# Products of every tile pair taken one pair later, with seven products for pair 0 as well, in an adaptive FFN kernel on one core

## The reference, cut to what matters

```python
# x: (32, 64, 1024) = 2048 tokens; W: (1024, 1024); A, B: 8 experts of rank 16; U, V: (1024, 256); S: (256,)
logits = x @ Wr.T + 5.0 * one_hot(ids)                     # 8 experts
gates  = softmax of the two largest logits, put at their places
h      = einsum('btd,erd->bter', x, A)
cond   = x @ W.T + 2.0 * einsum('bter,bte,eor->bto', h, gates, B)
out    = x + cond @ (U * S @ V.T).T
```

## Time and profile before

| | us |
|---|---|
| median of 3 executions | 155.24 (155.18 to 155.56) |
| the profiled execution, its own time | 154.92 |
| its span, first to last instruction | 153.1 |
| TensorE busy in the span | 148.8 (97%) |
| VectorE, GpSimd, ScalarE busy | 102.5, 67.2, 62.9 |

### The profile page before, as it was taken

How to read it: one execution, slowest core, us unless ns; L and a number is a source line. 1 busy time by engine, 2 the same in 40 slices (tenths; PEclk the granted TensorE clock), 3 DMA queues, 4 the chain that set the end, 5 groups by cost and what they waited for, 6 DMA issues and landing times.

```text
span 153.1 us, 2896 instructions
## 1 busy us (share of the span) xinstructions
PE 148.8 (97%) x1059; PEld 140.4 (92%) x1059; DVE 102.5 (67%) x291; ACT 62.9 (41%) x139; POOL 67.2 (44%) x53
## 2 busy tenths in 40 slices
PE   7999999999999999999999999999999999999991
PEld 5899999999998899899989998999899999989880
DVE  0787896945739997864884488267917782786551
ACT  4758783658626612812360335124511631230100
POOL 2000326015296650099129904970695089309000
PEclk9999999999999999999999999999999999999999
DMA  5999999996240059826198639765810680061084
GB/s 169 379 407 404 399 409 412 409 404 249 81 122 19 0 168 348 250 100 234 48 330 256 195 137 293 235 161 217 284 51 0 274 274 4 4 274 66 25 314 143
DMA packets 10669, 32.72 MB, mean 214 GB/s; under 512 B 1440, under 2 KB 1952, under 8 KB 10528
## 3 DMA queue, kind: packets, MB, share of 16 engines
q1 hardware_dynamic: 10368, 31.96, 58.1%
q10 hardware_dynamic: 288, 0.59, 1.0%
HBM read 24.16 MB, written 8.39 MB: 213 GB/s over the span
## 4 chain that ended last, share of the span: by engine, by line
PE 97%; DVE 0%; issue 0%; POOL 0%; DVEq 0%; POOLq 0%
PE fin L325 13%; PE fin L326 13%; PE fin L327 13%; PE pj L326 10%; PE pj L325 10%; PE pj L327 10%; PE zt L326 6%; PE zt L325 6%; PE zt L327 6%; PE fin L502 2%; PE gt L413 1%; PE zt L396 1%; PE fin L342 1%; PE gt L326 1%; PE gt L327 1%; PE gt L325 1%
## 5 line engine op out<-in xcount | busy, mean ns | idle before, releaser
L285 POOL TENSOR_TENSOR xT_lo<-xt_raw,xT_hi 128x1024 fp32r<-128x1024 f32 x16 | 38.2, 2407 | 67.3 <-DVE gh L762 32.9
L325 PE MATMUL pj<-proj_hi,xT_hi 128*128 128x264 f32 x128 | 36.4, 284 | 0.0
L326 PE MATMUL pj<-proj_lo,xT_hi 128*128 128x264 f32 x128 | 36.3, 284 | 0.0
L327 PE MATMUL pj<-proj_hi,xT_lo 128*128 128x264 f32 x128 | 36.2, 283 | 0.0
L325 PE MATMUL fin<-v_hi,w_hi 128*128 128x256 f32 (+1 forms) x84 | 26.4, 314 | 0.0
L326 PE MATMUL fin<-v_lo,w_hi 128*128 128x256 f32 (+1 forms) x84 | 26.3, 314 | 0.0
L327 PE MATMUL fin<-v_hi,w_lo 128*128 128x256 f32 (+1 forms) x84 | 26.3, 313 | 0.0
L300 POOL TENSOR_TENSOR x_all<-x_all,vw_raw 128x512 f32<-128x512 f32 x18 | 23.0, 1312 | 6.6 <-DVE vw_raw L810 6.6
L326 PEld LDWEIGHTS pj<-proj_lo,xT_hi 128*128 128x128 f32 x128 | 24.1, 188 | 0.2
L325 PEld LDWEIGHTS pj<-proj_hi,xT_hi 128*128 128x128 f32 x128 | 24.1, 188 | 0.2
L327 PEld LDWEIGHTS pj<-proj_hi,xT_lo 128*128 128x128 f32 x128 | 24.0, 188 | 0.0
(11 more groups left out here) (93 smaller groups left out, 288.0 us busy)
## 6 DMA issues: line engine op xcount, KB each, us to landing
xt_raw<-in_xt SPq DMA_DIRECT2D x16, 512.0 KB, 4.4
x_all<-in_x SPq DMA_DIRECT2D x16, 512.0 KB, 4.5
out<-x_all SPq DMA_DIRECT2D x13, 512.0 KB, 3.6
vw_raw<-in_VW SPq DMA_DIRECT2D x6, 384.0 KB, 7.0
w_raw<-in_W SPq DMA_DIRECT2D x8, 256.0 KB, 6.0
out<-x_all SPq DMA_DIRECT2D x5, 256.0 KB, 2.0
w_raw<-in_U SPq DMA_DIRECT2D x1, 1024.0 KB, 7.2
aw_raw<-in_AW SPq DMA_DIRECT2D x1, 544.0 KB, 7.2
```

Of the source, the lines that this page charges most:

```text
L285: nc.gpsimd.tensor_sub(xT_lo[:, t % XTR, :, :], xt_raw[:, t % XTR, :, :], xT_hi[:, t % XTR, :, :].bitcast(F32)).then_inc(xt_lo, 1)
L325: nc.tensor.matmul(dst, l_hi, r_hi, start=first, stop=False, skip_group_check=shared)
L326: nc.tensor.matmul(dst, l_hi, r_lo, start=False, stop=False, skip_group_check=shared)
L327: return nc.tensor.matmul(dst, l_lo, r_hi, start=False, stop=last, skip_group_check=shared)
```

## The change

All products move one pair later. While pair p runs, TensorE now issues `first_part(p-2)` between the two projections and `second_part(p-2)` after the second, then `half_t(p)` and `transpose_gh(p)`; `mix(p)` stands inside `project(2p+2)`, after five of its eight steps. Pair 0 has seven products like the others, so its `sums` and its differences of U S are needed too. At the end `first_part(6)`, `mix(7)` and `second_part(6)` follow the last `transpose_gh`, with `mix(7)` behind p1 and p6. The other engines' lists follow, and in the head the splits of x, B and U S stand at other places.

```diff
         LAST = TILES - 1
         PAIRS = TILES // 2
-        FAST = PAIRS - 2
-        HEAD_PRODS = 2 * HALF
+        LAG = 4
...
-                    if t == 2 and k == MH:
-                        mix(0)
+                    if t >= 2 and t % 2 == 0 and k == MH:
+                        mix(t // 2 - 1)
...
             for p in range(1, PAIRS):
                 project(2 * p)
-                if p >= 3:
+                if p >= 2:
+                    first_part(p - 2)
+                project(2 * p + 1)
+                if p >= 2:
                     second_part(p - 2)
-                project(2 * p + 1)
-                if p == 1:
...
-                    expand(0, bank_a, 0, 0, BANK)
-                    expand(0, bank_b, 0, BANK, D)
-                    pe.wait_ge(zb_lo, 1)
-                    expand(0, bank_c, MC, 0, BANK)
-                    expand(0, bank_d, MC, BANK, D)
-                else:
-                    first_part(p - 1)
-                transpose_gh(p)
                 zt_free(p)
                 half_t(p)
-                mix(p)
+                transpose_gh(p)
 
             p = PAIRS - 2
             q = (PAIRS - 1) % 2
+            p1(p)
+            p6(p)
+            mix(PAIRS - 1)
+            p7(p)
+            p5(p)
+            p2(p)
             second_part(p)
...
             split_x(0)
+            pool.wait_ge(w_lo_done, 2 * OC)
             split_x(1)
             split_x(2)
+            split_x(3)
+            pool.wait_ge(y_done, MC)
+            make_tsum(0)
+            make_tsum(1)
+            pool.wait_ge(gh_done, 2)
+            make_tsum(2)
+            make_tsum(3)
+            pool.wait_ge(tl_done, 1)
+            split_x(4)
             pool.wait_ge(us_lo_done, MC)
-            split_x(3)
-            for j in range(4):
-                make_tsum(j)
-            for p in range(1, PAIRS):
+            split_x(5)
+            for p in range(2, PAIRS):
+                if p < PAIRS - 1:
+                    split_x(2 * p + 2)
+                sides(p - 2)
...
             def pair(p):
+                if p >= 2 and p < PAIRS - 1:
+                    split_x(2 * p + 2)
                 split_za(p - 1)
...
+                copy_x22(p - 1)
                 copy_z(2 * p)
                 exp_top(2 * p)
+                if p >= 2:
+                    copy_u(p - 2)
+                split_zb(p - 1)
...
             def pair(p):
+                split_zb(p - 2)
+                if p == 2:
+                    split_us(1)
                 split_za(p - 1)
...
+                sums(p - 1)
...
                 gates_top(2 * p)
                 gates_apply(2 * p)
+                up(p - 2, 1)
+                up(p - 2, 2)
+                xb1(p - 2)
+                xa0(p - 2)
                 gates_top(2 * p + 1)
                 gates_apply(2 * p + 1)
...
+                xb0(p - 2)
+                xa1(p - 2)
+                split_gh(p)
...
             p = PAIRS - 2
+            split_zb(p)
+            up(p, 1)
             split_za(PAIRS - 1)
```

More of the change, by code:

```diff
@@ L240, in _ @@
             sp.dma_start(u_raw, U).then_inc(u_load, 16)
-            for t in range(XR):
+            load_xt(XTR)
+            for t in range(LAG):
                 load_x(t)
-            for p in range(PAIRS):
+            load_xt(XTR + 1)
+            for t in range(LAG, XR):
+                load_x(t)
+            for p in range(1, PAIRS):
+                if 2 * p + XTR < TILES:
+                    load_xt(2 * p + XTR)
+                    load_xt(2 * p + 1 + XTR)
                 if 2 * p >= XR:
@@ L604, in copy_x22 @@
             def copy_x22(p):
-                if p >= 2:
+                if p >= 1:
                     act.wait_ge(zb_lo, p)
@@ L690, in _ @@
             split_us(1)
-            split_x(3)
             split_gh(0)
-            for p in range(1, PAIRS):
+            split_x(4)
+            split_za(0)
+            copy_x22(0)
+            split_t(1)
+            copy_z(2)
+            exp_top(2)
+            split_zb(0)
+            split_x(5)
+            copy_z(3)
+            exp_top(3)
+            split_gh(1)
+            for p in range(2, PAIRS):
                 pair(p)
+            copy_u(PAIRS - 2)
             split_za(PAIRS - 1)
@@ L890, in _ @@
             gates_apply(1)
-            split_us(1)
             split_gh(0)
-            for p in range(1, PAIRS):
+            split_t(0)
+            split_za(0)
+            sums(0)
+            gates_top(2)
+            gates_apply(2)
+            gates_top(3)
+            gates_apply(3)
+            split_t(1)
+            split_gh(1)
+            for p in range(2, PAIRS):
                 pair(p)
             p = PAIRS - 2
+            split_zb(p)
+            up(p, 1)
             split_za(PAIRS - 1)
+            up(p, 2)
+            split_zb_plain(PAIRS - 1)
+            xb1(p)
+            xa0(p)
             xb0(p)
-            split_zb_plain(PAIRS - 1)
             xa1(p)
-            residual_end(HEAD_PRODS, bank_b, LAST - 1, 0, BANK)
-            residual_end(HEAD_PRODS + 1, bank_a, LAST - 1, BANK, D)
-            residual_end(HEAD_PRODS + 2, bank_c, LAST, 0, BANK)
-            residual_end(HEAD_PRODS + 3, bank_d, LAST, BANK, BANK + BANK // 2)
-            residual_end(HEAD_PRODS + 4, bank_b, LAST, BANK + BANK // 2, D)
+            residual_end(0, bank_b, LAST - 1, 0, BANK)
+            residual_end(1, bank_a, LAST - 1, BANK, D)
+            residual_end(2, bank_c, LAST, 0, BANK)
+            residual_end(3, bank_d, LAST, BANK, BANK + BANK // 2)
+            residual_end(4, bank_b, LAST, BANK + BANK // 2, D)
 def kernel(**inputs):
```

182 lines of the change are left out of this document (68 added, 114 removed).

## The result

The median is **160.35 us** (six executions, 159.14 to 160.46), against 155.21 of the kernel before beside it (154.83 to 155.56): a ratio of 1.0312, 95% interval 1.0293 to 1.0332. The forecast was 159.2. The six values lie in two places: two executions, at full mean clock, took 159.14 and 159.21; three with a mean granted clock of 0.989 took 160.44 to 160.46; one more took 160.26 at full mean clock. The profiled execution is one of the three at 0.989: 160.45, span 158.6, which is 5.5 more than the span of before.

What follows compares the result with a forecast made beforehand. TensorE's never-waiting list was taken as the bound: -0.68 (product) + 0.7 (A) + 2.4 (B) + 0.4 (C) + 1.2 (D) = +4.0, from 155.24 to 159.2 us. Own range 157.9 to 159.9; 157.0 to 160.6 given 0.80.

Steps and rivals of the forecast that it cites:

- A: Before the z transposes of pair 1, TensorE waits for ScalarE's copy_z(3): 0.7 us, bounds 0 and 0.9.
- B: During pair 2, before p2 of pair 0, TensorE waits for copy_u(0), delayed by held VectorE work: 2.4 us.
- C: In pairs 3 to 7, before p2, TensorE waits for copy_u: 0.08 us a pair, 0.4 in all.
- D: At the end, before p6 of pair 6, TensorE waits for VectorE's split_zb(6): 1.2 us, bounds 1.0 and 1.4.
- one product less: Pair 0 takes 7 products in place of 8, taking 0.68 us off TensorE's list.
- The thin point: In pair 2, GpSimd's split of tile 6 holds VectorE's dtop: wait 2.4 us, or 1.0 if not held.
- the first rival: In pair 2, dtop is not held: B is 1.0, the sum +2.6, time 157.9 us; chance 0.13.
- the second: Rival: the lock misses these places; A 0, B 0.1, C and D stay; +1.0, 156.3 us; chance 0.08.
- the third: Rival: all TensorE waits are covered and only the product counts: a gain, 154.6 us; chance 0.06.
- T: The start of a pair's first projection on TensorE, from which later times in the pair are counted; 51.1 in pair 2.
- The fifth rival: In pairs 3 to 7, C is larger, 0.3 us a pair: +1.1, time 160.3 us; chance 0.06.
- the fourth rival: TensorE's clock falls to its lower level in B, losing 1.7 us: time 160.9 us; chance 0.06.

Runs made afterwards that it cites:

- all four edits: Changed kernel with copy_u before copy_z, tile 6's GpSimd split behind tile 4's gates, split_zb(6) before last split_gh, copy_z(3) and exp_top(3) before tile 5's split: 154.37 us.
- six copies: Kernel with all four edits plus six idle ScalarE copies ahead of copy_u(0), so TensorE waits before p2 of pair 0: 161.66 us, ratio 1.0416 to before.

## Why the prediction was right, and where it was wrong

**The mechanism of the waits was right.** "TensorE's own list is the time" held: at full clock the changed kernel's 159.14 and 159.21 are the kernel with all four edits, 154.37, plus A 0.52, B 2.46, C 0.55 and D 1.23, which gives 159.13. The third execution at full clock, 160.26, is not covered by this. The terms beside the forecast:

| term | forecast | measured |
|---|---|---|
| one product less | -0.68 | -0.69 (all four edits against before) |
| A | 0.7 | 0.52 in the trace and by its edit |
| B | 2.4 | 2.46 |
| C | 0.4 | 0.55 |
| D | 1.2 | 1.23 in the trace, 1.1 to 1.4 by its edit |
| lower clock behind B | 0 | 1.4 in the trace, 1.3 between medians of the two places |

**How GpSimd holds VectorE.** The thin point was `dtop`, one row of 484 ns. It is now a row of 1.62 us that becomes 0.23 when GpSimd is idle beside it, so the first rival (157.9) falls, and so do the second and the third, in which the lock misses or all waits are covered. By the Trainium skill, SBUF — State Buffer, section "SBUF: two separate sides", an operation with one tensor input is held only in a two-port mode. The trace's 1.62 agrees with it if `dtop` runs in such a mode, which no row here names.

**C was mis-sized by 0.03 a pair**, and in kind: `copy_u` is late for the load of weights only, and the price is the slow first matmul behind it, 0.34 in place of 0.227. The sums of this wait end at T + 4.90 by the prediction's own rows, not 4.87, a slip of 0.03 that changes nothing. The fifth rival's 0.3 a pair did not come; that the median lies beside its 160.3 is chance.

**The step that failed is the clock behind wait B**, which the sum left out and the fourth rival had at too small a chance. The text said "No row shows TensorE idle later, so neither side has evidence", and gave the fall 0.06. But the forecast itself made TensorE idle for 2.4 us, and its own row of slow matmuls behind idleness was evidence for the side that has it fall. At waits of 2.0 to 3.1 the fall came in 18 of 30 executions of five kernels, in the changed kernel in 3 of 6, so the median went to 160.35: inside the range of 157.0 to 160.6, outside the forecast's own, 157.9 to 159.9. Longer matmuls behind a wait were among the prediction's own signs of being wrong, and the profiled execution has them. Where exactly the median lies is luck: with three executions of six fallen it is the mean of 160.44 and of the one at 160.26, which no trace explains. The price of the fall was near: 1.7 forecast, 1.3 measured. The Trainium skill, TensorE: Matmul & The Clock Gate, section "What's actually happening", says of a kernel's start that the number of slow matmuls differs between runs of the same kernel. The runs here show a like scatter behind a wait in the middle: slow matmuls in some executions of a kernel, none in others.

## What to carry to other kernels

When a kernel's bound engine never waits, a reordering is priced place by place: when is each operand delivered, and what stands ahead of it on the delivering engine's list? Three exchanges on an engine's list and one added wait on GpSimd turned 3% slower into 0.4% faster. The two that gave most: put the copy that the bound engine waits for ahead of a step whose releaser can be late, and hold GpSimd's long SBUF work back until VectorE's short chain is through, where the bound engine waits for that chain. A new wait of 2 us or more on TensorE also asks for a second number, what it costs if the clock falls behind it.

## What the hardware showed that was not expected

- The clock may fall after the wait has ended. In the changed kernel TensorE resumes at 59.47, does three 512-column and six 264-column steps, and is slow from about 61.0 until 64.4; with six copies it is slow from the first matmul on, for 5.6 us.
- The same kernel falls in one execution and not in the next when the wait is 2.0 to 3.1 us. D, a wait of 1.1 us, brought no fall in any trace.
- A weight load that is late by about 0.3 us leaves no wait on TensorE's own row, but a first 512-column matmul of 0.34 in place of 0.227.
- The head scatters: the same matmul of the first half-z stage started at 38.08 with `copy_u` first and at 38.96 with `copy_z(3)` moved, edits that lie behind it. That is more than wait A is worth, and A could be timed only with the other three waits gone.
